# A gated delta-rule layer with mixture-of-experts on one core: first leaf read from PSUM in pieces, one gram bank moved to the chunk's end, reciprocal deviations spread by DMA, and part of the output rows added on GpSimd

## The reference, cut to what matters

```python
def step(S, t):
    q_t, k_t, v_t, a_t, b_t = t
    y = jnp.einsum('bhvk,bhk->bhv', S, k_t)
    err = y - v_t
    S = a_t[..., None] * S - (b_t[..., None] * err)[..., None] * k_t[:, :, None, :]
    o = jnp.einsum('bhvk,bhk->bhv', S, q_t)
    return (S, o)
...
_, o = jax.lax.scan(step, S0, xs)
...
mu = jnp.mean(o, axis=-1, keepdims=True)
var = jnp.mean(jnp.square(o - mu), axis=-1, keepdims=True)
o = (o - mu) * jax.lax.rsqrt(var + LN_EPS) * ln_g + ln_b
g = jax.nn.sigmoid(x @ Wg).reshape(b, t, H, D)
o = (o * g).reshape(b, t, H * D)
return o @ Wo
```

## Time and profile before

| what | value |
| --- | --- |
| median of 3 runs (lowest to highest) | 3099.18 us (3096.86 to 3108.7) |
| span of the profiled execution, from its first to its last instruction | 3102.6 us |
| mean granted TensorE clock | 0.976 of full speed |
| busy: PE, DVE, ACT, POOL | 88%, 72%, 52%, 44% of the span |
| DMA | 84 GB/s in the mean |

### The profile page before, as it was taken

The page is one execution under the profiler, slowest core; times in us unless marked ns, Lnnn a source line. Parts: engine busy times, 40 slices in busy tenths (PEclk is TensorE's granted clock), DMA queues, the critical chain, the costliest instruction groups (busy, mean ns, idle before and its releaser), DMA issues. The chain is left out here.

```text
span 3102.6 us, 48417 instructions
## 1 busy us (share of the span) xinstructions
PE 2732.2 (88%) x14144; PEld 1863.5 (60%) x14144; DVE 2239.8 (72%) x4680; ACT 1610.3 (52%) x3516; POOL 1377.8 (44%) x1760
## 2 busy tenths in 40 slices
PE   7999999768898888988889888898888888859999
PEld 3555555446666666666666666666666666635555
DVE  6777777677888878888788887888887888623332
ACT  6666666545555555555555555555555555412111
POOL 3666676734544445444454444544445444310000
PEclk9999999989999999999999999999999999979999
DMA  3655556533232232322323223232223222034120
GB/s 124 241 225 206 233 230 239 196 82 67 43 57 42 44 65 47 57 42 43 64 49 57 42 44 59 53 57 42 44 51 61 46 53 43 9 107 109 45 38 14
DMA packets 449883, 261.22 MB, mean 84 GB/s; under 512 B 402672, under 2 KB 414672, under 8 KB 447472
## 3 DMA queue, kind: packets, MB, share of 16 engines
...
...
## 5 line engine op out<-in xcount | busy, mean ns | idle before, releaser
L265 DVE SCALAR_TENSOR_TENSOR A_acc<-A_psY,A_w,A_acc 128x410 f32<-128x410 f32 (+1 forms) x720 | 419.2, 637 | 151.6 <-ACT A_acc L334 151.6
L405 PE MATMUL A_psY<-A_xT,A_w 128*128 128x413 f32 (+1 forms) x960 | 347.2, 510 | 9.1 <-PE A_psAG L411 7.7
L1244 ACT ACTIVATE B_PQ<-B_psM 128x64 f32<-128x64 f32 (+2 forms) x480 | 125.2, 261 | 441.2 <-DVE B_NC L1137 440.9
L1137 DVE TENSOR_TENSOR B_NC<-B_NC,B_psM 128x256 f32<-128x256 f32 x480 | 200.8, 418 | 182.5 <-PE B_psM L1756 92.8
L192 POOL TENSOR_TENSOR A_outs<-A_outs,A_acc 128x410 f32<-128x410 f32 (+1 forms) x240 | 229.7, 987 | 216.1 <-ACT A_outs L342 216.1
L899 POOL TENSOR_TENSOR B_WT<-B_WT,B_G 128x128 f32<-128x128 f32 (+2 forms) x224 | 143.4, 640 | 371.2 <-ACT B_WT L1244 184.3
L1244 ACT ACTIVATE B_WL<-B_psT 64x128 f32<-64x128 f32 (+3 forms) x480 | 148.5, 309 | 265.6 <-PE B_psT L1723 265.4
L405 PEld LDWEIGHTS A_psY<-A_xT,A_w 128*128 128x128 f32 x960 | 180.2, 189 | 165.5 <-issue 164.2
L1140 DVE TENSOR_REDUCE B_W<-B_NC 128x64 f32<-128x320 f32 x512 | 248.7, 486 | 17.6
L334 ACT ACTIVATE A_acc<-A_psY,A_w 128x410 f32<-128x410 f32 (+1 forms) x240 | 166.1, 692 | 162.9 <-PE A_psY L405 161.2
L879 POOL TENSOR_TENSOR B_PQ<-B_PQ,B_G 128x256 f32<-128x256 f32 x128 | 89.4, 699 | 345.5 <-DVE B_WT L1105 345.5
(11 more groups left out here) (207 smaller groups left out, 6588.4 us busy)
## 6 DMA issues: line engine op xcount, KB each, us to landing
...
A_xc<-nbeta SPq DMA_DIRECT2D x16, 1024.0 KB, 5.9
...
```

The source lines that it names most:

```text
L265: nc.vector.scalar_tensor_tensor(a, y, w[:, s, col:col + 1], a, ALU.mult, ALU.add)\
L405: last = nc.tensor.matmul(psY[p][:, y0:y0 + HALO + t1 - t0], wp[:, p, kt, :], xT[:, kt, t0:t1 + HALO], start=kt == 0, stop=kt == KT - 1)
L1137: tt(eq[:, :, :, 1:5], eq[:, :, :, 1:5], left.unsqueeze(2).to_broadcast([128, H, R, R]), ALU.mult)\
L1244: copy = lambda out, in_: nc.scalar.activation(out, in_, ACT.Copy)
```

## The change

- **First leaf.** `first_leaf` on DVE multiplies each quarter of the heads straight from its contact bank and sums after the second and the fourth. ACT's copy of a bank now waits for DVE's piece of it (`ap`).
- **Split gram.** Gram 3 of chunk g + 1 is made at the end of chunk g, one product before and one after the state updates (`next_gram`), and ACT masks it behind `w_rows_copy`. The mask of gram 2 stands behind leaf 0's WL copy.
- **Reciprocals.** `dev` and `rstd` leave PE. ACT's `deviation` moves from leaf 12 to leaf 11, ahead of that leaf's WL copy. DVE inverts the 8 x 128 tile in place, SP stores it to DRAM and, when that has landed, loads it back as 512 KB spread over all partitions into SQ. `norm` multiplies by SQ in place of a PSUM bank. FQ may be written again once `norm` is done.
- **Own terms.** POOL adds two rows of WX to each half of FQ (`add_own_terms`), `oc` waits for that and has one 512-column product less per half. `decayed_q` 0 to 2 move one place later in POOL's order.
- **Smaller.** Leaf 15 is written straight to WE, so ACT's last copy to WE takes 3 leaves in place of 4. Three semaphores of the first stage are merged into one that counts to three.

```diff
-        -1: [("gram", 2), ("gram", 3)],
+        -1: [("gram", 2)],
...
-        12: ([("gram", 0)] if not last else []) + ([("dev", 0)] if out else []) + ([("wo_rest", 0)] if wo else []),
+        12: ([("gram", 0)] if not last else []) + ([("wo_rest", 0)] if wo else []),
         13: [("decay", 2), ("decay", 3)],
-        14: [("ktok", 1)] + ([("rstd", 0)] if out else []) + ([("wo_rest", 1)] if wo else []) + ([("rstd", 1)] if out else []),
+        14: [("ktok", 1)] + ([("wo_rest", 1)] if wo else []),
...
+            def spread_rstd(o):
+
+                wait(sp, rd, o, 1)
+                wait(sp, rld, o, 0)
+                sp.dma_start(rstd_d, sdev[:]).then_inc(rst.sem, 16)
+                wait(sp, rst, o, 1)
+                sp.dma_start(FQ, rstd_d.rearrange("i x -> (i x)").partition_broadcast(128)).then_inc(rld.sem, 16)
...
                     load("C0", n, at)
+                if g:
+                    spread_rstd(g - 1)
...
-                wait(pool, sd, o - 1, 1)
+                wait(pool, on, o - 1, 2)
                 tt(FQ.rearrange("p (r l h n) -> p r l h n", r=R, l=2, h=H)[:, n], by_row(Qs[o % 2])[:, n],
                    E[:, o % 2, F_ + n].rearrange("p h (n l) -> p l h n", l=2), ALU.mult).then_inc(fq.sem, 1)
+
+            def add_own_terms(o, half):
+
+                wait(pool, yv, o, half + 1)
+                wait(pool, fq, o, 2 * half + 2)
+                x = FQ[:, 512 * half:512 * (half + 1)].rearrange("p (k x) -> p k x", k=2)
+                tt(x, x, WX[:, 4 * half:4 * half + 3:2], ALU.add).then_inc(own_sum.sem, 1)
...
                 scale_right(g, 3)
+                past(g, 1)
+                scale_left(g, 1)
                 if g:
                     decayed_q(g - 1, 0)
-                scale_left(g, 1)
-                past(g, 1)
-                if g:
-                    decayed_q(g - 1, 1)
                 past(g, 2)
                 if g >= 2:
                     gate(g - 2, 0)
                     gate(g - 2, 1)
                 if g:
-                    decayed_q(g - 1, 2)
+                    decayed_q(g - 1, 1)
                 if more:
                     row_decays(g + 1, 0)
                     row_decays(g + 1, 1)
                 past(g, 3)
                 if g >= 2:
                     gate(g - 2, 2)
+                if g:
+                    decayed_q(g - 1, 2)
+                    add_own_terms(g - 1, 0)
                 past(g, 4)
                 scale_right(g, 5)
                 scale_left(g, 3)
                 past(g, 5)
                 if g:
                     decayed_q(g - 1, 3)
+                    add_own_terms(g - 1, 1)
...
             def invert(o):
-                ps = take_bank(dve, o + 1, "dev", 0)
-                nc.vector.reciprocal(rdev[:], ps[:, 0:8]).then_inc(rd.sem, 1)
+                wait(dve, sd, o, 1)
+                nc.vector.reciprocal(sdev[:], sdev[:]).then_inc(rd.sem, 1)
 
             def norm(o, i):
-                ps = take_bank(dve, o + 1, "rstd", i)
+                wait(dve, rld, o, 1)
                 x = O[:, 8 * i:8 * (i + 1), :]
-                tt(x, x, ps[:].rearrange("p (h c) -> p h c", h=8), ALU.mult).then_inc(on.sem, 1)
+                tt(x, x, SQ[:, 8 * i:8 * (i + 1), :], ALU.mult).then_inc(on.sem, 1)
...
+            def first_leaf(g, eq):
+
+                for n in range(4):
+                    h = slice(4 * n, 4 * n + 4)
+                    left = take_bank(dve, g, "contact", n)[:].rearrange("p (h q t) -> p h q t", h=4, q=2)[:, :, at_p(g), 0:R]
+                    tt(eq[:, h, :, 1:5], eq[:, h, :, 1:5], left.unsqueeze(2).to_broadcast([128, 4, R, R]), ALU.mult)\
+                        .then_inc(ap.sem, 1)
+                    if n == 1:
+                        wait(dve, awm, g - 1, 3)
+                        wait(dve, wxc, g - 1, 1)
+                    if n % 2:
+                        half = slice(8 * (n // 2), 8 * (n // 2) + 8)
+                        wait(dve, ap, g, n + 1)
+                        nc.vector.tensor_reduce(W[:, half, 0:R], eq[:, half], AXIS.X, ALU.add).then_inc(ws.sem, 1)
...
+                        wait(dve, tps, g, 12)
+                        to = WE[:, :, R * j:R * (j + 1)]
...
+                    wait(act, ap, g, i + 1)
                     copy(pair(g)[:, :, 4 * i:4 * i + 4, :], ps[:].rearrange("p (h q t) -> p q h t", h=4, q=2)).then_inc(cont.sem, 1)
...
                     elif j == 11:
                         if more:
                             pairs_copy(nxt)
+                        if g:
+                            deviation(g - 1)
...
+                    if j == 0:
+                        mask_gram_act(g, 2)
...
-                wait(act, wt, g, J)
+                wait(act, wt, g, JM)
                 wait(act, wsc, g, JM // 2)
                 wait(act, wsc0, g, JM // 2 + 1)
-                copy(w_end(12, J), w_leaves(12, J)).then_inc(wec.sem, 1)
+                copy(w_end(12, JM), w_leaves(12, JM)).then_inc(wec.sem, 1)
...
+                if more:
+                    wait(act, mps, g, 16)
+                    mask_gram_act(g + 1, 3)
...
+                    wait(pe, own_sum, g - 1, n + 1)
                     mm(ps[:], center[:], FQ[:, 512 * n:512 * (n + 1)], start=True, stop=False)
-                    mm(ps[:], center[:], WX[:, 4 * n:4 * n + 3:2], start=False, stop=False)
                     if n:
+                        mm(ps[:], center[:], WX[:, 3:6:2], start=False, stop=False)
                         return
...
-                elif kind == "dev":
-                    wait(pe, sd, g - 1, 1)
-                    last = nc.tensor.transpose(ps[:, 0:8], sdev[:], ident[0:8, 0:8])
-                elif kind == "rstd":
-                    wait(pe, rd, g - 1, 1)
-                    for m in range(4):
-                        i = 4 * n + m
-                        last = nc.tensor.transpose(ps[:, 128 * m:128 * (m + 1)],
-                                                   rdev[:, i:i + 1].to_broadcast([128, 128]), ident[:])
...
+            def next_gram(g, part):
+
+                if g + 1 == NCH:
+                    return
+                ps, filled = open_bank(pe, g, "gram", 3) if part == 0 else (ring[place[g, "gram", 3][0]], full[place[g, "gram", 3][0]])
+                if part == 0:
+                    loaded(pe, "KB", g + 1)
+                    loaded(pe, "Q", g + 1)
+                    wait(pe, kc, g + 1, 2)
+                (j, i), (bank, col) = [item for item in grams.items() if item[1][0] == 3][part]
+                p, w_, r0 = merge_of(j)
+                hp = 128 // w_
+                left = KC[:].rearrange("p n c -> p (n c)")[:, 256 + 128 * i:][:, 0:128]
+                last = mm(ps[:, col:col + 256], left, KQ[:, (g + 1) % 2, 1:3, i * hp:(i + 1) * hp, r0:r0 + w_], start=True, stop=True)
+                if part:
+                    last.then_inc(filled, 1)
...
                 wait(pe, yv, g - 1, 3)
-                mm(ps[:], center[:], WX[:, 3:6:2], start=False, stop=False)
                 mm(ps[:], center[:], WX[:, 7:9], start=False, stop=False)
...
+                next_gram(g, 0)
                 for i in range(4):
                     run_job(g, ("update", i))
+                next_gram(g, 1)
...
```

More of the change, by code:

```diff
@@ L246, in _ @@
                 tap[p].start(dve)
-            c_used[0].start(dve)
-            c_used[1].start(dve)
             with dve.Fori(0, TURNS) as t:
@@ L390, in _ @@
             pe.wait_ge(beta_sb, T // 512)
-            w_used[0].start(pe)
-            w_used[1].start(pe)
             with pe.Fori(0, TURNS) as t:
@@ L458, in chunk_jobs @@
     if g < 0:
-        return [("own", 0, 0), ("own", 0, 1), ("kk", 0, 0), ("kk", 0, 1), ("gram", 0)]
+        return [("own", 0, 0), ("own", 0, 1), ("kk", 0, 0), ("kk", 0, 1), ("gram", 0), ("gram", 3)]
     if g == NCH:
-        return [("qk", n, l) for n in range(3) for l in range(2)] + [("oc", 0), ("oc", 1), ("var", 0), ("dev", 0), ("rstd", 0), ("rstd", 1)]
+        return [("qk", n, l) for n in range(3) for l in range(2)] + [("oc", 0), ("oc", 1), ("var", 0)]
     if g > NCH:
@@ L466, in chunk_jobs, with last_chunk @@
         jobs += [job for job in short_jobs(g, j) + leaf_jobs(g, j) if job[0] not in ("oc_rest", "wo_rest")]
-    return jobs + [("update", i) for i in range(4)]
+    return jobs + [("update", i) for i in range(4)] + ([("gram", 3)] if not last_chunk(g) else [])
+def last_chunk(g):
+    return g + 1 == NCH
 JOBS = [(g, *job) for g in range(-1, NCH + 2) for job in chunk_jobs(g)]
@@ L757, in _ @@
                 loaded(sp, what, NCH - 1)
+            wait(sp, rst, NCH, 0)
+            wait(sp, rld, NCH, 0)
             wait(sp, ldc, NCH, 0)
@@ L965, in _ @@
                 decayed_q(NCH - 1, n)
+            for half in range(2):
+                add_own_terms(NCH - 1, half)
             for n in range(4):
@@ L1570, in shared_job @@
                 elif kind == "gram":
-                    gi = g if n else g + 1
```

(8 more changed lines are left out.)

73 lines of the change are left out of this document (34 added, 39 removed).

## The result

The changed kernel takes 3156.4 us (median of 4 executions, 3147.4 to 3156.7), the kernel before 3098.8 (4 executions, 3096.9 to 3108.7): ratio 1.0177, 95% interval 1.0160 to 1.0194. The forecast was 3130, with a range of 3075 to 3160. The sign and the range held, and 26 us were missing. The profiled execution of the changed kernel is the shortest of its four, 3147.4 us with a span of 3145.7.

The account below looks back on a forecast made before the run. The prediction took DVE's queue in the leaf loop, with DVE and POOL sharing an SBUF port, as the bound. +0.85 us a chunk gave 26 over 31, -1.0 first chunk, +5.8 at the end: 3130 us, range 3075 to 3160.

Parts of the forecast that it names:

- first leaf: Chunk start: WR ready up to 1.0 us sooner, partly lost to waits for POOL's late decayed_w; 0.45 us gained a chunk.
- first addition: Leaf 4: POOL's addition holds DVE's multiply into WR through the shared SBUF port; 0.6 us lost a chunk.
- second addition: Leaf 6: POOL's addition delays scale_right, which holds a DVE instruction before leaf 7; 0.6 us lost a chunk.
- reciprocal: Leaf 13: DVE's 128-column reciprocal takes about 0.86 us and makes leaf 14 late; 0.5 us lost a chunk.
- chunk end: End of chunk: PE drops eight transposes, odd chunks save 0.85 us, even ones 0.1; mean 0.45 us gained.
- Own terms: Leaves 4 and 6: POOL's two additions of about 1.2 us hold DVE, 0.6 us lost each per chunk.
- Reciprocals and round trip: Leaf 13 loses 0.5 us a chunk; the transfer costs nothing within chunks, 5.8 us more behind the last chunk.
- B: Whole kernel faster, 3075 us: full first-leaf gain, POOL waits mostly beside DVE's idle time, reciprocal costs 0.1; chance 0.23.
- C: Whole kernel unchanged, 3104 us: port lock in leaf 4 only (0.6 us), reciprocal 0.3; chance 0.15.
- D: A late transfer holds norm ahead of the state additions, 24 us on top of A: 3154 us; chance 0.12.
- A: Likeliest case, whole kernel slower as the terms sum; own range 3116 to 3150 us; chance 0.50.
- the root and the second product: ACT's root ahead of leaf 11's WL copy and the second gram product ahead of the contact: 0.05 us lost together.

Follow-up runs that it names:

- a4_leaf_only: The kernel before with only the first leaf in pieces and the first stage's merged semaphore: 3099.6 us, ratio 1.0000 to the kernel before.
- a3_neither: The changed kernel with both POOL's additions and the reciprocals' DRAM round trip undone; first leaf in pieces, WE and split gram stay: 3093.8 us.
- a1_no_own: The changed kernel without POOL's own-term additions, products whole on PE again, POOL in its former order: 3110.2 us.
- b1_pe_busy: The changed kernel with eight unread transposes added on PE behind leaf 14's key tokens in even chunks: 3133.5 us.
- c4_no_filler: The changed kernel without POOL's additions and with the reciprocal moved from leaf 13 to leaf 11, no unread transposes: 3075.0 us.
- a2_pe_rstd: The changed kernel with the reciprocals through PE and PSUM as before, no DRAM round trip; POOL's additions stay: 3144.3 us.
- b2_no_own_pe_busy: The changed kernel without POOL's additions, with eight unread transposes on PE in even chunks: 3086.0 us.
- c1_grams_behind: a3_neither with both products of the next chunk's gram behind the state updates: 3071.6 us.

## Why the prediction was right in sign and 26 us short

The mechanisms stand in order in the chunk, so each can be read from the stretch it acts on. These are differences of after against before in us, as means of the even and of the odd chunks from 2 to 30, worked out from the starts of the contacts and of each leaf's multiply (lines 1137 and 1174):

| stretch | forecast | even | odd |
| --- | --- | --- | --- |
| contact to leaf 1 (first leaf) | -0.45 | -0.46 | -0.99 |
| leaf 4 to 5 (first addition) | +0.6 | +0.71 | +0.69 |
| leaf 6 to 7 (second addition) | +0.6 | +0.67 | +0.74 |
| leaf 13 to 14 (reciprocal) | +0.5 | +0.48 | +0.42 |
| leaf 15 to the next contact (chunk end) | -0.1 even, -0.85 odd | +1.83 | -0.88 |
| whole chunk, with 0.05 forecast for the rest | +1.2 even, +0.45 odd | +3.20 | -0.15 |

One term is off by much: the end of the even chunks, by 1.93 us, which is 31 us in 16 chunks. The first leaf of the odd chunks gave 0.54 us more than taken, 8 us in 15. The others were right or nearly so.

By whole kernels, undone one behind the other, the parts are: the first leaf 0 (a4_leaf_only against before), the chunk's end -6 (a3_neither), reciprocals and round trip +16 (a1_no_own), additions +46 (the changed kernel).

- **Chunk end: the step that failed.** The prediction had the eight transposes as work that TensorE is rid of, "in even ones the stretch lies in waits and the shorter last copy to WE gives 0.1 us". In even chunks they were what TensorE did in those waits. Without them it is idle there, the granted clock falls to the 1.2 GHz level at the end of 15 of 15 even chunks instead of 9, and the updates, which set the end, take 3.15 us for 2.06. Instead of the 0.1 us gained, 1.83 were lost. b1_pe_busy shows cause and price: the same number of transposes, read by no one, bring 1.69 us of it back in each even chunk and 23 us in all, and c4_no_filler shows it again in another kernel. In the odd chunks the gain was there as forecast (-0.88 for -0.85): the end has 1.04, 0.60 and 2.06 us without a gap.
 That the clock follows how busy the engine has been is in the Trainium skill too ("TensorE: Matmul & The Clock Gate", section "Part 1: The HAM clock gate (the "warmup" mystery)"); the prediction drew on it nowhere.
- **Own terms.** Forecast 1.2 us a chunk, 37 in all, and 1.2 behind the last chunk. The profiles give 1.38 in even and 1.43 in odd chunks, some 44; the kernels 46 (a1_no_own) and 50 (a2_pe_rstd against a3_neither). The mechanism was right in both leaves, and each addition takes 1.27 us for the 1.2 estimated. Each wait was some 0.1 us above the 0.6 taken, well inside its bounds.
- **Reciprocals and round trip.** Forecast 15.5 + 5.8 = 21, measured 16. In leaf 13 the term was right (0.48 and 0.42 for 0.5), and so was the duration (0.93 for 0.86; the lower bound of 0.3 took 1 ns a column from sums that take 486 ns for 320 columns, which is 1.5, but nothing hangs on it). Behind the last chunk it is 6.8 us, for the 8.4 of the sum, and the end of the span is 3.3 us later for 5.8. The 16 are a net of two large parts that the forecast hadn't: a1_no_own has even chunks 2.21 us longer than a3_neither and odd ones 1.69 shorter. In the even ones that is the reciprocal (0.69), a later leaf 1 (0.48) and a longer end (0.95; the unread transposes of b2_no_own_pe_busy take 1.43 off it); in the odd ones the end is 2.08 us shorter. c1_grams_behind shows that the bank which `norm` holds is part of those 2.08; how they divide between the bank and the transposes wasn't tried.
 From the Trainium skill's repeat count ("VectorE: DVE Perf Modes", section "First, the fixed hardware budget") 1.2 us had been estimated; 0.93 was measured.
- **First leaf.** Forecast -0.45 of 1.0 us a chunk, held by POOL's last decayed_w. The even chunks have just that, with `scale_leaf` held (0.80 us, 0.29 where nothing holds it); the odd ones gave the whole 1.0, and so did all chunks of a3_neither (0.94), where `norm` reads PSUM. That the forecast named 0.45 for every chunk and met it in half of them is in part luck. By whole kernels the leaf is worth 0 alone and 52 us in another kernel: the size was a property of what stands around it, above all of the gram ahead of leaf 0, as the prediction had said, and of whether the leaf reads SBUF beside POOL, which it had not.
- **Rivals.** B and C are out. D gave 3154, next to the median, but not by its mechanism: `norm` waits for no transfer in the chunks. A was the right case, and its own range of 3116 to 3150 ended 6 us too low, by the clock. That 3156 lies in the stated range owes something to the width that D's transfer gave it, a mechanism that didn't act.
- The forecast 0.05 for the root and the second product, and nothing for the first stage's semaphore, weren't tried by themselves; a4_leaf_only has the merged semaphore beside the first leaf, and its time doesn't differ from before.
